# A graph network's prologue on Trainium2: the layer norm's mean, root and shift made by GpSimd, and VectorE's statistics spread through the index chain

## What is computed

```python
N, E, D = 50000, 100000, 128
def layernorm(x):                       # over the 128 features
    return (x - x.mean(-1)) / sqrt(x.var(-1) + 1e-5)
h = relu(layernorm(x))                  # this one is in the part that is changed
for l in range(3):
    agg = segment_sum(h[src], dst) / max(deg, 1)
    h = leaky_relu(agg @ Wl[l].T + b[l] + h @ Wr[l].T, 0.01)
x = x + h
h = relu(layernorm(x)) @ W              # second block, done with phase 3
a_s, a_d = h @ att_src, h @ att_dst
e = leaky_relu(a_s[src] + a_d[dst], 0.2)
alpha = softmax of e over the edges of each dst
out = x + segment_sum(h[src] * alpha, dst) + bias
```

## Time and profile before

| | |
|---|---|
| Time of the kernel, median of 3 runs | 2480.31 us |
| lowest and highest of the 3 | 2474.58 and 2480.49 us |
| Time of the profiled execution | 2483.16 us |
| its span, from first to last instruction | 2481.4 us |
| DVE busy in the span | 1993.1 us (80%) |
| PE busy | 1863.2 us (75%) |
| POOL busy | 1604.0 us (65%) |
| ACT busy | 1393.1 us (56%) |

### The profile page before, as it was taken

How to read it: one execution, slowest core, us unless ns; L and a number is a source line. 1 busy time by engine, 2 the same in 40 slices (tenths; PEclk the granted TensorE clock), 3 DMA queues, 4 the chain that set the end, 5 groups by cost and what they waited for, 6 DMA issues and landing times. The chain is left out here.

```text
span 2481.4 us, 49369 instructions
## 1 busy us (share of the span) xinstructions
PE 1863.2 (75%) x12384; PEld 1624.2 (65%) x12384; DVE 1993.1 (80%) x8196; ACT 1393.1 (56%) x3699; POOL 1604.0 (65%) x1662
## 2 busy tenths in 40 slices
PE   0000788989886788888878999999999566666665
PEld 0000677878775677777767888888888455566555
DVE  7987766666664666666667999999999699999999
ACT  3688344444442232222233666666666689898987
POOL 2011777777775777777757776666663577777774
PEclk9999999999998999999998999999999699998999
DMA  6686688888886888888877888888888488787876
GB/s 197 211 283 238 205 256 245 263 256 256 252 256 183 248 257 253 253 258 252 257 230 204 264 260 251 252 253 254 252 253 238 138 206 208 206 208 203 210 200 179
DMA packets 596345, 579.67 MB, mean 234 GB/s; under 512 B 78763, under 2 KB 556581, under 8 KB 596032
## 3 DMA queue, kind: packets, MB, share of 16 engines
q1 hardware_dynamic: 402272, 337.58, 45.0%
q0 software_dynamic: 52672, 109.59, 20.2%
q10 hardware_dynamic: 141120, 129.32, 15.2%
HBM read 369.23 MB, written 207.75 MB: 233 GB/s over the span
## 5 line engine op out<-in xcount | busy, mean ns | idle before, releaser
L635 POOL DMA_INDIRECT rows<-tab,idx x1215 | 1194.0, 983 | 558.0 <-issue 310.3
L852 PE MATMUL bank<-mask,rows 128*128 128x128 f32 (+1 forms) x3528 | 642.0, 319 | 182.7 <-DMA rows<-tab,idx 159.9
L852 PEld LDWEIGHTS bank<-mask,rows 128*128 128x128 f32 x3528 | 542.1, 194 | 256.7 <-issue 137.7
L1268 DVE TENSOR_TENSOR sage<-bank,sage 128x256 f32<-128x256 f32 x588 | 247.2, 420 | 383.8 <-PE bank L852 382.0
L722 ACT ACTIVATE sage<-bank,b_col 128x256 f32<-128x256 f32 x392 | 185.9, 474 | 571.5 <-PE bank L878 570.7
L635 POOL DMA_INDIRECT rows<-tab_c,idx x405 | 388.2, 959 | 181.7 <-issue 108.8
L1248 DVE TENSOR_SCALAR mask<-iota,dcol 128x256 f32<-128x256 f32 (+1 forms) x1215 | 415.3, 371 | 0.1
L953 PE MATMUL bank<-ident,mask 128*128 128x128 f32 x784 | 138.0, 302 | 159.2 <-ACT mask L782 158.6
L1274 DVE TENSOR_TENSOR sage<-sage 128x256 f32<-128x256 f32 x588 | 247.2, 420 | 1.6 <-DMA sage<-inv_d 1.3
L1279 DVE SCALAR_TENSOR_TENSOR sage<-sage 128x256 f32<-128x256 f32 x588 | 242.8, 413 | 4.6 <-ACT sage L722 4.6
L877 PE MATMUL bank<-sage,wcat 128*128 128x256 f32 x784 | 236.7, 384 | 0.0
(11 more groups left out here) (219 smaller groups left out, 3359.6 us busy)
## 6 DMA issues: line engine op xcount, KB each, us to landing
sage<-inv_d SPq DMA_DIRECT2D x588, 128.0 KB
turned<-sage ACTq DMA_DIRECT2D x392, 128.0 KB
tab<-sage ACTq DMA_DIRECT2D x392, 128.0 KB
sage<-turned SPq DMA_DIRECT2D x392, 128.0 KB, 4.0
tab_c<-sage ACTq DMA_DIRECT2D x196, 132.0 KB
own_w<-tab_c SPq DMA_DIRECT2D x196, 132.0 KB, 2.7
tab<-sage SPq DMA_DIRECT2D x49, 512.0 KB, 3.4
xin<-tab SPq DMA_DIRECT2D x196, 128.0 KB
```

Source lines behind the costliest of these rows:

```text
L635: eng.indirect_dma_start(out=rows[:, s.win[w], 0:width], out_offset=None, in_=table, in_offset=bass.IndirectOffsetOnAxis(ap=idx[:, s.w + w ...
L852: m = eng.matmul(to[:, a:b], rows[:, s.win[w], 0:D], mask[:, s.mw[w], c:c + b - a], start=(w == 1), stop=(w == 2))
L1268: eng.tensor_tensor(agg_t[:, o.r, :], ps[:, 0:TILE], own_t[:, o.v, :], ALU.add).then_inc(S["sum_v"], 1)
```

## The change

For the first layer norm alone, DVE keeps only `bn_stats`, written to a ring of four groups (`LNR` = 4). These statistics hold, for the even and the odd elements of each block, the mean and the sum of squared deviations. A new function of POOL's program, `moments`, makes of the halves the reciprocal root and the shift in ten instructions of 128x8: two sums and a difference, three scalings, the difference squared, added, the power -0.5, and the product for the shift. ACT has no square root here any more. DVE's new `groups(n)` puts single groups and pairs inside the chain's steps, so that 27 groups stand before `net_v` (19 before). POOL's `moments` stand between its gathers at places that are given by a small table, `AT`.

```diff
+LNR = 4
+AT = {"rows": 3, "net": 27}
...
+            def moments(a, b):
+                for g in range(a, b):
+                    r = g % LNR
+                    of = st_g[:, r, :, :]
+                    d, t, m, rs, nm = half_d[:, r, :], half_s[:, r, :], half_m[:, r, :], rstd_g[:, r, :], nmr_g[:, r, :]
+                    eng.wait_ge(S["bn_v"], g + 1)
+                    eng.tensor_tensor(d, of[:, :, 1], of[:, :, 4], ALU.subtract)
+                    eng.tensor_tensor(m, of[:, :, 2], of[:, :, 5], ALU.add)
+                    eng.tensor_tensor(t, of[:, :, 1], of[:, :, 4], ALU.add).then_inc(S["ln_v"], 1)
+                    eng.wait_ge(S["ln_v"], g + 1)
+                    eng.tensor_scalar(d, d, 0.5, None, ALU.mult)
+                    eng.tensor_scalar(m, m, 1.0 / D, 1e-5, ALU.mult, ALU.add)
+                    eng.tensor_scalar(t, t, -0.5, None, ALU.mult).then_inc(S["ln_a"], 1)
+                    eng.wait_ge(S["ln_a"], 3 * g + 1)
+                    eng.tensor_tensor(d, d, d, ALU.mult).then_inc(S["ln_a"], 1)
+                    eng.wait_ge(S["ln_a"], 3 * g + 2)
+                    eng.tensor_tensor(m, m, d, ALU.add).then_inc(S["ln_a"], 1)
+                    eng.wait_ge(S["ln_a"], 3 * g + 3)
+                    wait(eng, S["h_a"], g - LNR + 1)
+                    eng.tensor_tensor(rs, m, power[:, :], ALU.pow).then_inc(S["rs_v"], 1)
+                    eng.wait_ge(S["rs_v"], g + 1)
+                    eng.tensor_tensor(nm, t, rs, ALU.mult).then_inc(S["nmr_v"], 1)
...
+            moments(0, AT["rows"])
             eng.wait_ge(S["prep_v"], 2)
...
+            moments(AT["rows"], AT["net"])
             eng.wait_ge(S["net_v"], 1)
...
+            moments(AT["net"], AT["net"] + 1)
             eng.wait_ge(S["pk_st"], 16)
...
+                if k % 3 == 2:
+                    moments(AT["net"] + 1 + k // 3, AT["net"] + 2 + k // 3)
+            moments(AT["net"] + 3, NSG)
             eng.wait_ge(S["flag_rdy"], 1)
...
-                if g < NSG:
-                    eng.wait_ge(S["ln_v"], g + 1)
-                    eng.activation(std[:, g % 2, :], mv[:, g % 2, :, 1], ACT.Sqrt, bias=eps[:, 0:1]
-                                   ).then_inc(S["ln_a"], 1)
...
+                eng.wait_ge(S["nmr_v"], g + 1)
+                for j in range(GJ):
+                    a = eng.activation(x_g[:, g % GR, j * D:(j + 1) * D], x_g[:, g % GR, j * D:(j + 1) * D],
+                                       ACT.Relu, bias=nmr_g[:, g % LNR, j:j + 1], scale=rstd_g[:, g % LNR, j:j + 1])
+                a.then_inc(S["h_a"], 1)
...
+            def groups(n):
+                for g in range(done[0], done[0] + n):
+                    eng.wait_ge(S[f"xg{g % GR}"], 16 * (g // GR + 1))
+                    wait(eng, S["ln_v"], g - LNR + 1)
+                    for j in range(GJ):
+                        m = eng.bn_stats(st_g[:, g % LNR, j, :], x_g[:, g % GR, j * D:(j + 1) * D])
+                    m.then_inc(S["bn_v"], 1)
+                done[0] += n
...
             for b in range(MOVES):
                 close_up(word, b)
                 if b < MOVES - 1:
-                    groups(12 + b, 13 + b)
+                    groups(1 + b % 2)
+            reached("net")
             eng.sem_inc(S["net_v"], 1)
...
-            groups(29, NSG)
-            scale_g(NSG - 1)
+            groups(NSG - done[0])
```

More of the change, by code:

```diff
@@ L300, in build @@
         mask = sb("mask", [P, MRING, TILE])
[L301 to L305, removed]
+        bst = sb("bst", [P, 2, 6])
+        mv = sb("mv", [P, 2, 2, 2])
+        st_g = sb("st_g", [P, LNR, GJ, 6])
+        half_d = sb("half_d", [P, LNR, GJ])
+        half_s = sb("half_s", [P, LNR, GJ])
+        half_m = sb("half_m", [P, LNR, GJ])
+        rstd_g = sb("rstd_g", [P, LNR, GJ])
+        nmr_g = sb("nmr_g", [P, LNR, GJ])
+        power = sb("power", [P, GJ])
+        std = sb("std", [P, 2, 2])
+        rstd = sb("rstd", [P, 2, 2])
+        nmr = sb("nmr", [P, 2, 2])
         own_c = own_w[:, :].rearrange("p (r j c) -> p r j c", r=DEEP, j=2)
@@ L574, in gpsimd_program @@
             eng.memset(g_node[:, D:D + 1], 1.0).then_inc(S["low_g"], 1)
+            eng.memset(power[:, :], -0.5).then_inc(S["low_g"], 1)
+            eng.wait_ge(S["low_g"], 12)
+            def moments(a, b):
[20 more added lines that the diff above has]
+                    eng.tensor_tensor(nm, t, rs, ALU.mult).then_inc(S["nmr_v"], 1)
             eng.wait_ge(S["prep_v"], 1)
@@ L655, in weights @@
                 eng.activation(wg[:, D:D + 2], bank[0][:, 0:2], ACT.Copy).then_inc(S["wg_cp"], 1)
-            for g in range(NSG + 1):
-                if g == GAHEAD:
+            for g in range(NSG):
+                if g == GAHEAD - 1:
                     weights()
-                if g < NSG:
-                    eng.wait_ge(S["ln_v"], g + 1)
-                    eng.activation(std[:, g % 2, :], mv[:, g % 2, :, 1], ACT.Sqrt, bias=eps[:, 0:1]
-                                   ).then_inc(S["ln_a"], 1)
[L664 to L671, removed]
+                eng.wait_ge(S["nmr_v"], g + 1)
[3 more added lines that the diff above has]
+                a.then_inc(S["h_a"], 1)
             eng.wait_ge(S["flag_rdy"], 1)
@@ L1027, in vector_program, with reached @@
             eng.sem_inc(S["prep_v"], 1)
[L1029 to L1057, removed]
+            done = [0]
+            def groups(n):
[6 more added lines that the diff above has]
+                done[0] += n
+            def reached(name):
+                assert done[0] == AT[name], (name, done[0])
+            groups(3)
+            reached("rows")
             eng.wait_ge(S["row_ld"], 32)
@@ L1066, in vector_program @@
             eng.sem_inc(S["prep_v"], 1)
-            groups(1, 3)
+            groups(2)
             eng.wait_ge(S["src_ld"], 16)
@@ L1074, in vector_program @@
             op(eng.tensor_reduce(stat[0:NAT_P, 1:2], cmp_n[:, :], AX.X, ALU.add))
+            groups(1)
             op(eng.tensor_tensor(cmp_m[:, :], s_nat[:, :], d_nat[:, :], ALU.not_equal))
@@ L1077, in vector_program @@
             op(eng.tensor_reduce(stat[0:NAT_P, 2:3], cmp_m[:, :], AX.X, ALU.add))
-            groups(3, 5)
+            groups(2)
             eng.wait_ge(S["run_ld"], 64)
@@ L1099, in vector_program @@
             eng.sem_inc(S["chain_v"], 1)
-            groups(8, 10)
+            groups(1)
             op(eng.scalar_tensor_tensor(w_a[:, :, :], run_s[:, :, 0:RUN], float(TILE), drel[:, :, :],
@@ L1126, in vector_program @@
             eng.sem_inc(S["flag_v"], 1)
-            groups(10, 12)
+            groups(1)
             op(eng.tensor_copy(fill5[:, :], lead[:, :]))
@@ L1154, in vector_program @@
             op(eng.tensor_tensor(flag[:, :], flag_f[:, 0:1], flag_f[:, 2:3], ALU.mult))
-            groups(19, 25)
+            groups(6)
             off_k = lead[:, :].unsqueeze(2).to_broadcast([HALF, HWIN, P])
@@ L1169, in vector_program @@
             op(eng.scalar_tensor_tensor(dst_f[:, :, :], dst_f[:, :, :], 1.0, filled[:, :, :], ALU.add, ALU.mult))
+            groups(1)
             op(eng.tensor_tensor(src_f[:, :, :], filled[:, :, :], src_i[:, :, :], ALU.mult))
             eng.sem_inc(S["end_v"], 1)
-            groups(25, 29)
+            groups(3)
             eng.wait_ge(S["ix_ps"], 1)
```

11 lines of the change are left out of this document (6 added, 5 removed).

## The result

The change made the kernel slower: 2509.12 us by the median of four runs (2507.11 to 2513.98), against 2479.59 for the kernel before beside it. The ratio is 1.0126, 95% interval 1.0106 to 1.0147: 29.5 us lost where 38.6 were forecast as gained. The profiled execution took 2507.11 us (span 2505.4), 24 us above that of before; it is the fastest of its four, and that of before lies above all of its timed runs, so that the medians differ by more.

What follows compares the result with a forecast made beforehand. The prologue was taken as bounded first by DVE, last by ACT, its delay carried through. Last store 36.0 us earlier plus 2.6 from gathers, 38.6 off 2483.16, gave 2444.6; less 2.85 to the median, 2442 us. Range 2430 to 2496.

Steps and rivals of the forecast that it cites:

- the power is a further unknown: GpSimd's group: the power on eight columns taken as 0.15 us, three times DVE's reciprocal price by column.
- the power is computed lane by lane: Rival on GpSimd's group: a power of 1.5 us gives 2490 us, one of 2.5 gives 2535; chance 0.21.
- 78 + 45p: Prologue's end: time of the last table store if GpSimd, at p over 3.1 us a group, bounds the last stretch.
- One gain more: Prologue's end: DVE's second network starts earlier, no longer waiting for the last square root; spared slow gathers save 2.6 us.
- held time: Index chain before the hand-over: DVE's long network instructions hold GpSimd up, 27 us taken from between 0 and 47.5.
- A late start: Start of GpSimd's 24 groups, put at 34.7: last edge gather starting at 33.46, plus 1.25 us.
- late x: Early groups: three in DVE's 7.93 us wait cost nothing if x arrives in time; late x would prove the forecast wrong.
- all 47.5 us of chain: Blocking rule pushed to the whole chain: hand-over at 139.8, last store 20.5 us later than forecast.
- Landing and windows: Behind the hand-over: 0.4 us issue, 3.97 packed store and landing, 8.9 for seven window gathers; 13.3 us.
- The table load in phase 3: ACT in phase 3: one table load more, between nothing and 3.08 us, counted as nothing because ACT has room.

Runs made afterwards that it cites:

- the experiment with the wait: The changed kernel, with VectorE's second network waiting for the last group's shift: 2884.71 us, ratio 1.0084 to the kernel before.
- With the product: The changed kernel with the power replaced by a product, reciprocal root left out: 2839.87 us, ratio 0.9929 to the kernel before; 2839.19, 0.9928 in a later set.
- the version with one early group: The changed kernel with a product for the power, one group instead of three ahead of the row search: 2465.66 us, ratio 0.9928 to the kernel before.
- the product and the network behind the last shift: The changed kernel with a product for the power and the second network waiting for the last shift: 2457.59 us, ratio 0.9902 to the kernel before.

## Why the prediction was wrong

**The step that failed** is the one on the power: "the power is a further unknown", costed from DVE's reciprocal at 0.15 us. It measured 1.67. The nine others with their waits took 2.29 (the forecast had 2.25 for ten), so p, GpSimd's time for a group, was 3.96 and not 2.4, above the 3.53 from which, by the prediction, the change loses. The rival "the power is computed lane by lane" had the price (1.5 us) and the side, and got 0.21. A row of another engine's other operation could not price it: the text itself said that no row bounded it from above. Put p = 3.96 into its formula, 78 + 45p, and the last store is at 256, which makes some 2500 us: this one term takes the time out of the stated range. The row says 276. The rest, by rows:

- *A count.* 3 + 24 + 3 groups leave 19, and the formula for a GpSimd bound took 18: 4.0 us.
- *"One gain more".* The earlier network was to spare 2.6 us of slow gathers. It did (8.1 us back), but it ran beside POOL's last groups and cost 16.6; with another 1.7 of holding around 181 us, 18.3. The sign of this step was wrong, and the experiment with the wait shows it. The forecast had counted held time only for the index chain.
- *A late start.* POOL's run of 24 groups began at 39.77 and not at 34.7: 5.1. The prediction named late x as a danger, but x is only a part of it. DVE's offsets for the edge gathers were out 2.0 us later than before, behind the late x. POOL then took 2.0 us more because its own third early group, with the power in it, ran until 33.15, and its four edge gathers, beside DVE's long instructions, were spread over 1.2 us more (0.2 came back behind them). With the product, where x was late too (5.0 and 5.2 us for the second group), the run began at 35.0 and 35.1. And as the version with one early group shows, the early places still pay.

```profile
31.17 0.17 DVE L1090 CAST start_i<-e_first 98x2 int32<-98x2 f32 x1
...
33.73 1.10 POOL L629 DMA_INDIRECT run_s<-edges,start_i  x1 [0.59 <-issue]
```

- *Held beside the chain.* 24 groups took 115.9 us (39.77 to 155.65), 20.8 above 24 x 3.96; the 27 were 6.2 too many. The Trainium skill (SBUF — State Buffer, section "Who interferes with whom") states that a VectorE instruction with two SBUF inputs, or in a two-port mode, that has started first blocks a reading GpSimd instruction for its whole length, and the rows on held instructions above agree in kind. To push this to all 47.5 us of chain was the prediction's own reading, and it is far from these 20.8.
- *Landing and windows.* 155.65 to 179.30 is 11.8 without the three groups, not 13.3: 1.5 less, since a group now hides in the landing.

256.2 + 4.0 + 18.3 + 5.1 - 6.2 - 1.5 + 0.4 at the end gives 276.3; the row says 276.4.

**What held.** DVE kept eight statistics of 1.64 us, no more. ACT's group without the root is 3.08 us (55.48 for 18). The table load in phase 3 took 1.28 us and has nothing to show in a total. And slow gathers are spared when the network stands earlier, 8.1 us of them.

**Even with a cheap power the forecast was too good.** With the product and the network behind the last shift p was 2.49, near the 2.4, and yet the last store left at 214.95 and not at 198.3. The packed store was at 130.8 and not at 119.7. POOL's rows separate these 11 us: its 24 groups took 95.5 us (34.98 to 130.49), of which 59.8 are 24 x 2.49, 10.9 are waits for DVE's statistics at five places, and 24.8 are held time. The forecast had 57.6, nothing and 27. So the held time was about right, and what was missing is the waits. The longest of them stands behind DVE's longest wait for x, which the prediction had only as a danger for the early groups. Two things can make x late. The list of waits up to 135 us has SP waiting at 16 loads of x for a table store to land, since a slot is loaded again only then (last line), and the loads issued up to 70 us took 4.1 to 19.4 us to land. Which weighs more was not tested.

```profile
51.75 1.65 DVE L1074 BATCH_NORM_STATS2 st_g<-sage 128x6 f32<-128x128 f32 x8 [8.37 <-DMA sage<-in_x]
...
53.48 1.38 POOL L598 TENSOR_TENSOR half_d<-st_g 128x8 f32<-128x8 f32 x1 [6.32 <-DVE st_g L1074]
...
SPq L435 <- DMA tab<-sage: 39.6, 16, 10.2
```

Behind the packed store, landing, window gathers and three groups took 1.4 us more than forecast. Then POOL needed 6.8 us for two groups, partly held, before ACT ran unbroken from 159.1, with 18 groups left and not 19 (3.0 less). The gain that the mechanism is worth is thus some 20 to 26 us, not 38.6, and only without the power.

## What to carry to other kernels

An operation that no row shows on its engine has no price: bound the change by the break-even and ask what stands against being above it; "eight columns on another engine" did not. Then count every instruction moved to GpSimd twice, once free and once beside what VectorE runs there, and look at the end too, where a freed VectorE starts its next long work early and runs into the last of them. When a step is shortened on one engine, check what sets the pace next (here, in part, the loads into the seven slots of x).

## What the runs showed of the hardware

- GpSimd's power of 128x8 took 1.67 us and of 128x16 2.93; a product, sum or scaling of either 0.20 to 0.26. The price goes by column and is eight times that of a product at eight columns.
- Beside VectorE's network (COPY_PREDICATED of 1.6 us and integer TENSOR_SCALAR of 0.8 us in turn) most 0.2 us instructions of GpSimd end about when VectorE's ends, so ten take some 12 us (11.7 with the power, 12.0 with the product). Beside batch-norm statistics they keep their 0.2 us.
- On the slower chips the prologue's rows took the same (the power 1.67 us on both kinds), but from 300 to 500 us POOL issued 133 instructions in the kernel with the product, against 159 in the same kernel with the wait on the faster chip. The DMA engines moved 214 and not 255 GB/s there, and the granted clock was 0.95 and not 0.99. Which of these is the cause stays open; the kernel before takes 377 us more.
